# A merged out-projection and FFN head: turns set between products, masks in banks of their own, rows split ahead of the routing

## The chip, the cores and the metric

The kernel runs on one core of one Trainium2 chip. The metric is the device time of one launch in microseconds (us), as the median of several runs.

## The reference

Two transformer layers are computed over x of shape 4 x 512 x 512 (four batches of 512 tokens, width 512). Each layer is a cross-attention and a feed-forward block, each on a layer norm of x, with residual adds. This case touches the joint between the second layer's attention and its feed-forward block:

```python
attn = attn.reshape(b, n, N_HEADS * HEAD_DIM)
return attn @ Wout + bout                       # added to x
...
xf = layernorm(x).reshape(-1, d)
gate_base, up_base = xf @ Wg.T, xf @ Wu.T       # DFF = 1408
probs = softmax(xf @ Wr.T)                      # 8 experts
topw, topi = top_k(probs, 2)
# for each expert e, with weight we (zero where e is not chosen):
h = silu(gate_base + xf @ Ag_e.T @ Bg_e.T * 2) * (up_base + xf @ Au_e.T @ Bu_e.T * 2)
acc += (h @ Ad_e.T @ Bd_e.T * 2) * we           # rank 16
out = x + silu(gate_base) * up_base @ Wd.T + acc
```

## The kernel before

Each engine has its own list of instructions, written out by hand, and semaphores join the lists. A product of full precision is made from two halves: every operand is split in a high part (a copy by ACT, rounded to the type that TensorE reads) and a low part (a subtraction by DVE), and `product` runs three matmuls for each of four slices of the inner dimension, 12 in all, each 128x512. A block that must stand with its columns on the partitions is first "turned": four 128x128 transposes on TensorE into one PSUM bank, from which ACT and then DVE make the two halves.

The stage around the change is `phase_out_head`. A tile is 128 tokens; a batch has four tiles. The loop `for j in range(B + 2)` is a pipeline over the four batches:

- for batch j (while j < 4): `turn_rows` turns the four tiles of attention output, `row_hi` (ACT) and `row_lo` (DVE) split them into `aT`, `out_product` multiplies with Wout into the banks `y0` and `y1`, DVE adds to x (`add`) and takes statistics (`add_stats`, `variance`), ACT takes the root (`deviation`), DVE the `reciprocals`, and POOL writes the normalised rows (`normalise`) over `wout_raw`.
- for batch j-1: `turn_x`, `normed_hi`, `normed_lo` turn and split the normalised rows into `late_xnT`; `router` multiplies with Wr, `copy_router` and `turn_logits` bring the logits back to tokens on partitions, and `route` (DVE, 21 short instructions, with two exponentials of ACT, `gaps`, among them) picks the two experts and writes `hots`.
- for batch j-2: `turn_hots`, `hot_rows_hi` and `hot_rows_lo` turn that choice, `masks` spreads it by four small products to four masks of 128x512, ACT copies them (`copy_masks`), `lora_rows` multiplies the rows with Ag and Au into the banks `a0` and `a1`, DVE multiplies them with two of the masks (`mask_rows`), and ACT and POOL split the result (`masked_hi`, `masked_lo`).

With j = 4 and j = 5 no out-projection is left, and `prep` turns and splits the first slice of FFN weights at j = 4. The turns of rows and of x share the two banks `tp0` and `tp1`, and the masks of before use them too. The sync engine (SP) issues all DMAs of the stage in a fixed order. An all-engine barrier ends the stage, and `phase_ffn1` follows: 44 steps of matmuls over slices of DFF, whose products go through a ring of three banks and are summed by DVE into x and into `down_acc`, which lies in the memory of `attn`, and was first cleared there.

In the traces `attn` is also the memory of the attention rows, the masks, the masked rows and the raw weights; `late_weights` holds `aT`, `sel` and the turned choice besides the FFN weights; `wout_raw` holds the normalised rows.

## Time and profile before

| | |
|---|---|
| median of 3 runs | 1816.04 us (1815.12 to 1817.34) |
| profiled execution, its own time | 1813.96 us |
| its span | 1811.4 us |
| mean granted TensorE clock | 0.942 of full speed |
| TensorE busy over the span | 1632.4 us (90%) |
| VectorE (DVE), ScalarE (ACT), GpSimd (POOL) busy | 1059.8, 786.7, 460.1 us |
| `phase_out_head` in the trace | 1060.8 us to 1217.6 us |

The profile names a group by the line of the kernel, the engine, the operation and the tiles (out<-in). All products have line 48 or 56, the helpers, so they are told apart by their tiles: `h_y` is the out-projection, `h_a` the adapter rows, `h_r` the router, `h_tp` and `h_m` are turns and masks, `f_...` belongs to `phase_ffn1`. Idle time is given with what ended it.

### The profile page before, as it was taken

To read this page: it belongs to the slowest core of one execution; us is meant where nothing else is said; L and a number is where in the kernel's file an instruction comes from. 1 tells how busy PE (TensorE), PEld (TensorE's weight loads), DVE (VectorE), ACT (ScalarE), POOL (GpSimd) and SP (SyncE) were. 2 spreads that over 40 slices of the span, in tenths; PEclk is the share of its full clock that TensorE was granted. 3 is DMA by queue.
4 is the path that set the end of the run, shared out by engine and by line. 5 is a ranking of instruction groups with operands and counts; after the bars stand their busy time and mean duration, and the time that the engine had idled before them with its cause. 6 is when DMAs were issued, how large, how long until landed. Compare 5 with 4: busy or idle time off the path is not lost. (4 is left out here: it accounts for less than half of the span.)

```text
span 1811.4 us, 25116 instructions
## 1 busy us (share of the span) xinstructions
PE 1632.4 (90%) x8534; PEld 1197.8 (66%) x8534; DVE 1059.8 (59%) x1957; ACT 786.7 (43%) x1239; POOL 460.1 (25%) x425
## 2 busy tenths in 40 slices
PE   6988599999767869999999987969999999999996
PEld 5767599999745643343334355647888888888885
DVE  5886622222166748889998835534555556544545
ACT  4663223323244316877887852443333333223321
POOL 1210123322155650111110010242322232333331
PEclk9999599999978877999999998889999999999998
DMA  8995135562165572222222211332333336422211
GB/s 283 342 376 188 36 124 208 215 225 82 53 232 163 186 198 54 72 72 72 70 66 66 51 19 47 138 134 96 125 125 97 111 120 280 145 82 70 78 54 58
DMA packets 109515, 236.12 MB, mean 130 GB/s; under 512 B 39808, under 2 KB 53248, under 8 KB 100688
## 3 DMA queue, kind: packets, MB, share of 16 engines
q1 hardware_dynamic: 103152, 214.06, 35.1%
q0 software_dynamic: 6240, 20.45, 3.3%
q8 instruction: 73, 1.20, 0.3%
q14 instruction: 50, 0.41, 0.1%
HBM read 274.71 MB, written 93.32 MB: 203 GB/s over the span
## 5 line engine op out<-in xcount | busy, mean ns | idle before, releaser
L1937 DVE TENSOR_REDUCE r_top<-r_ring 128x1 f32<-128x512 f32 x512 | 324.1, 682 | 35.9 <-PE r_ring L1834 31.6
L1920 ACT ACTIVATE r_probs<-r_st 128x1024 f32<-128x1024 f32 x256 | 248.1, 1022 | 49.8 <-PE r_st L1821 47.3
L2824 DVE TENSOR_TENSOR attn<-attn,f_u 128x512 f32<-128x512 f32 x132 | 90.8, 688 | 193.9 <-PE f_u L48 133.5
L48 PE MATMUL m_bank<-w_place,m_xT 128*128 x936 | 168.1, 329 | 3.6 <-issue 1.7
L2750 ACT ACTIVATE attn<-f_g 128x512 f32<-128x512 f32 x132 | 79.0, 599 | 183.9 <-PE f_g L56 124.1
L48 PEld LDWEIGHTS m_bank<-w_place,m_xT 128*128 128x128 f32 x936 | 153.4, 191 | 7.8 <-issue 4.5
L1855 PE MATMUL r_out<-r_probs,early_v 128*17 128x512 f32 x1024 | 136.4, 605 | 0.5 <-ACT r_probs L1920 0.4
L2779 POOL TENSOR_TENSOR wout_split<-attn,wout_split 128x512 fp32r<-128x512 f32 x66 | 85.7, 1298 | 196.2 <-ACT wout_split L2754 196.2
L2779 POOL TENSOR_TENSOR f_hidS<-attn,f_hidS 128x512 fp32r<-128x512 f32 x66 | 85.6, 1297 | 194.8 <-ACT f_hidS L2754 194.8
L48 PE MATMUL f_g<-late_xnT,late_weights 128*128 128x512 f32 x528 | 129.5, 395 | 5.0 <-PEq L2064 5.0
L48 PE MATMUL f_u<-late_xnT,late_weights 128*128 128x512 f32 x528 | 129.4, 394 | 0.0
L1834 PE MATMUL r_ring<-early_slots 48*128 48x512 f32 x256 | 108.2, 507 | 17.5 <-PEq L1281 12.9
L2792 DVE TENSOR_TENSOR x_tokens<-f_ring,x_tokens 128x512 f32<-128x512 f32 x176 | 120.2, 692 | 0.0
L48 PEld LDWEIGHTS f_g<-late_xnT,late_weights 128*128 128x128 f32 x528 | 100.7, 191 | 26.4 <-issue 5.4
L48 PEld LDWEIGHTS f_u<-late_xnT,late_weights 128*128 128x128 f32 x528 | 97.7, 188 | 19.8
L1834 PEld LDWEIGHTS r_ring<-early_slots 48*128 48x128 f32 x256 | 44.9, 196 | 99.1 <-DVE r_top L1937 81.2
L1834 PE MATMUL r_ring<-r_kM,r_qS 48*128 48x512 f32 x256 | 104.8, 480 | 2.8 <-DVE r_top L1937 0.5
L1743 POOL TENSOR_TENSOR attn<-r_sums,r_rinv 128x256 f32<-128x256 f32 x32 | 19.9, 622 | 337.3 <-DVE r_rinv L1953 337.3
L1194 DVE TENSOR_TENSOR m_hT<-m_bank,m_hT 128x384 fp32r<-128x384 f32 x39 | 21.8, 558 | 137.8 <-ACT m_hT L1027 109.2
L1834 PEld LDWEIGHTS r_ring<-r_kM,r_qS 48*128 48x128 f32 x256 | 43.4, 189 | 86.4 <-DVE r_top L1937 79.8
L48 PE MATMUL m_bank<-w_place,m_hT 128*128 (+1 forms) x351 | 90.8, 403 | 1.4 <-DVE m_hT L1194 1.4
L834 POOL DMA_INDIRECT y_rows<-m_rows,m_scatter_at x39 | 38.6, 990 | 187.5 <-ACT m_rows L1034 187.5
(330 smaller groups left out, 3076.0 us busy)
## 6 DMA issues: line engine op xcount, KB each, us to landing
w_place<-expert_split SPq DMA_DIRECT2D x72, 1408.0 KB
w_place<-expert_split SPq DMA_DIRECT2D x36, 1024.0 KB
late_w_dram<-late_weights SPq DMA_DIRECT2D x11, 1920.0 KB
expert_split<-w_place SPq DMA_DIRECT2D x10, 1408.0 KB, 9.4
w_place<-expert_split SPq DMA_DIRECT2D x36, 384.0 KB
late_weights<-late_w_dram SPq DMA_DIRECT2D x11, 1024.0 KB
late_weights<-late_w_dram SPq DMA_DIRECT2D x11, 896.0 KB
early_slots<-y_rows SPq DMA_DIRECT2D x16, 512.0 KB
```

What stands on the lines that cost most here:

```text
L48: last = nc.tensor.matmul(out, l, r, start=(i == 0), stop=(i == len(passes) - 1))
L834: nc.gpsimd.indirect_dma_start(y_rows, bass.IndirectOffsetOnAxis(scatter_at[:, i:i + 1], 0), rows[:, XS + i % YS, :], None).then_inc(y_out ...
L1194: nc.vector.tensor_tensor(hT[:, i % 2, LO], bank[1][:, 0:FT * P].rearrange("p (j c) -> p j c", j=FT), fp32(hT[:, i % 2, HI]), ALU.subtract ...
L1743: nc.gpsimd.tensor_tensor(fp32(attn[:, b * KT:(b + 1) * KT, at:at + GROUP * HD]).rearrange("p t (h c) -> p t h c", h=GROUP), sums[g % 2][: ...
L1834: nc.tensor.matmul(ring(place(q, h))[:], qS[s][rows, h // 2, q * P:(q + 1) * P], kM[s][rows, h // 2, :], start=True, stop=True).then_inc(m ...
L1855: last = nc.tensor.matmul(out_ps[h * PAD:h * PAD + VCOLS, :], v[:, k, g, h * VCOLS:(h + 1) * VCOLS], probs[k][:, h, :], start=(k == 0), st ...
L1920: nc.scalar.activation(probs[k][:, 2 * pair:2 * pair + 2, :], st_ps[pair][:], ACT.Exp, scale=SCALE).then_inc(exp_done, 1)
L1937: nc.vector.reduce_max(top[g % 2][:, q, h:h + 1], ring(place(q, h))[:], AXIS_X).then_inc(max_read, 1)
L2750: nc.scalar.activation(hid[:, c, var, :], g_ps[c][:], ACT.Silu).then_inc(silu_done, 1)
L2779: nc.gpsimd.tensor_tensor(hidS[c][:, var, LO, :], hid[:, c, var, :], fp32(hidS[c][:, var, HI, :]), ALU.subtract).then_inc(hid_split, 1)
L2792: nc.vector.tensor_tensor(x[:, at, :], ring(use)[:], x[:, at, :], ALU.add).then_inc(y_added, 1)
L2824: nc.vector.tensor_tensor(hid[:, c, var, :], hid[:, c, var, :], u_ps[c][:], ALU.mult).then_inc(hid_done, 1)
```

## The change

Nothing is computed in another way, apart from the first sums of `down_acc`. What changes is the order in each engine's list, the banks of the masks, and some waits.

- The turns of x stand one by one between the products of the next batch, masks and adapter products instead of in a block of four, and the masks and the adapter rows of batch j-2 come before the router of batch j-1 instead of after it. At j = 5 the adapter rows come first.
- The masks use the banks `m` and `r` (which the turned choice and the router use) instead of `tp0`, `tp1` and `m`.
- `row_lo` for the first two tiles of the next batch stands ahead of `route` on DVE.
- The constants are turned after the second product of batch 0 instead of after the fourth.
- SP stores the masks of batch 2 ahead of the split weights, and no longer waits at the end of the stage for the masks to land; `phase_ffn1` waits for them instead, on SP before the first load of a mask and on ACT before its first step.
- In `phase_ffn1` the first sums into `down_acc` are written by a copy; the memset that cleared it is gone, and DVE's wait for it.

```diff
-        mask_ps = (tp[0], tp[1], m_ps, tp[0])
+        mask_ps = (m_ps, r_ps, m_ps, r_ps)
...
+            store_masks(2)
             sp.wait_ge(prep_split, late.PARTS)
             late.store_split(sp, 0)
-            store_masks(2)
             store_masks(3)
-            sp.wait_ge(mask_out, B * DMA)
...
# PE, turn_rows(j, t), t < 2
-                    wait_count(pe, mask_copied, 4 * (j - 2))
-                    wait_count(pe, x_split, TPB * (j - 1))
+                    wait_count(pe, rows_split, TPB * (j - 1) + t + 3)
+                    wait_count(pe, x_split, TPB * (j - 2) + t + 3)
# PE, turn_x(j, t), t < 2
-                    pe.wait_ge(rows_split, TPB * min(j + 2, B))
-                    if j + 1 >= B:
-                        pe.wait_ge(mask_copied, 4 * (j - 1))
+                    pe.wait_ge(rows_split, min(TPB * (j + 1) + t + 3, TILES))
+                    wait_count(pe, x_split, TPB * (j - 1) + t + 3)
# PE, router(j)
+                wait_count(pe, mask_copied, 4 * j)
# PE, masks(j, *ks)
-                        pe.wait_ge(x_split, TPB * min(j + 2, B))
-                        wait_count(pe, mask_copied, 4 * j)
-                    elif k == 3:
-                        pe.wait_ge(mask_copied, 4 * j + 1)
+                    elif k == 1:
+                        pe.wait_ge(logits_copied, j + 1)
+                    else:
+                        pe.wait_ge(mask_copied, 4 * j + k - 1)
...
# DVE, the loop's end at each j (before: route, row_lo, row_lo, mask_rows)
+                if routed:
+                    mask_rows(j - 2, 1)
+                if j == B:
+                    prep_lo(3)
                 if j + 1 < B:
                     row_lo(j + 1, 0)
                     row_lo(j + 1, 1)
-                if j >= 2:
-                    mask_rows(j - 2)
+                if normed:
+                    route(j - 1)
...
# ACT, the middle of the loop
+                if routed:
+                    copy_masks(j - 2, 0, 1)
+                if out_now:
                     deviation(j)
+                if j == B:
+                    prep_hi_of(1)
+                if normed:
+                    normed_hi(j - 1, 2)
...
# phase_ffn1
+            act.wait_ge(late.mask_out, B * DMA)
-            nc.gpsimd.memset(down_acc, 0.0).then_inc(acc_clear, 1)
...
-                nc.vector.tensor_tensor(acc, ring(use)[:], acc, ALU.add).then_inc(y_added, 1)
+                if step % STEPS_H < CH:
+                    nc.vector.tensor_copy(acc, ring(use)[:]).then_inc(y_added, 1)
+                else:
+                    nc.vector.tensor_tensor(acc, ring(use)[:], acc, ALU.add).then_inc(y_added, 1)
```

TensorE at j = 2, from the first product of batch 2 on, stands so before (`h_y` is a product of the out-projection, `h_tp<-identity,attn` a turn of attention rows, `h_tp<-identity,wout_raw` a turn of x, `h_m<-identity,h_hots` the turned choice):

```order
L48 MATMUL h_y1<-wout_split,late_weights 128x512 x12
L2178 MATMUL h_tp1<-identity,attn 128x128 x4
L48 MATMUL h_y0<-wout_split,late_weights 128x512 x12
L48 MATMUL h_y1<-wout_split,late_weights 128x512 x12
L2178 MATMUL h_tp0<-identity,wout_raw 128x128 x4
L2178 MATMUL h_tp1<-identity,wout_raw 128x128 x4
L2178 MATMUL h_tp0<-identity,wout_raw 128x128 x4
L2178 MATMUL h_tp1<-identity,wout_raw 128x128 x4
L2178 MATMUL h_m<-identity,h_hots 32x128 x4
L56 MATMUL h_r<-late_xnT,h_wrT 8x512 x12
```

and so in the changed kernel, from the third product to the turn that precedes the router:

```order
L48 MATMUL h_y0<-wout_split,late_weights 128x512 x12
L2177 MATMUL h_tp0<-identity,wout_raw 128x128 x4
L48 MATMUL h_y1<-wout_split,late_weights 128x512 x12
L2177 MATMUL h_tp1<-identity,wout_raw 128x128 x4
L2240 MATMUL h_m<-late_weights 128x512
L2240 MATMUL h_r<-late_weights 128x512
L48 MATMUL h_a0<-late_xnT,h_abT 128x512 x12
L2177 MATMUL h_tp0<-identity,wout_raw 128x128 x4
L2240 MATMUL h_m<-late_weights 128x512 x2
L2240 MATMUL h_r<-late_weights 128x512 x2
L48 MATMUL h_a1<-late_xnT,h_abT 128x512 x12
L2177 MATMUL h_tp1<-identity,wout_raw 128x128 x4
```

The four turns of x have moved apart, and the masks (L2240) and both adapter products (`h_a`) now stand among them, ahead of the router.

DVE behind the routing of batch 0, from the end of j = 1 into j = 2, stands so before (`h_hots` is the end of `route`, `late_weights<-h_tp` is `row_lo`, `x_tokens<-h_y` the add of a product):

```order
L2466 TENSOR_TENSOR h_hots<-ht_hot,ht_w 128x4x8
L2468 TENSOR_TENSOR h_hots<-ht_hot,ht_w 128x4x8
L2412 TENSOR_TENSOR late_weights<-h_tp,late_weights 128x512 x2
L2417 TENSOR_TENSOR x_tokens<-h_y,x_tokens 128x512
L2412 TENSOR_TENSOR late_weights<-h_tp,late_weights 128x512
```

and so in the changed kernel, from the last split of x at j = 1 to the start of `route` (its first line is the copy of the logits):

```order
L2478 TENSOR_TENSOR late_xnT<-h_tp,late_xnT 128x4x128
L2470 RECIPROCAL h_rstd<-h_std 128x4
L2472 SCALAR_TENSOR_TENSOR h_shift<-h_moments,h_rstd 128x4
L2478 TENSOR_TENSOR late_xnT<-h_tp,late_xnT 128x4x128 x2
L2449 TENSOR_TENSOR late_weights<-h_tp,late_weights 128x512 x2
L2488 COPY h_logits<-h_r 128x32
L688 TENSOR_REDUCE ht_top<-h_logits 128x4
```

The two splits of the next batch's rows, which stood between the end of the routing and the first add, now stand ahead of the routing's first copy, and the `reciprocals` have moved ahead of the last two splits of x.

TensorE at the end of the stage, from the last router on, stands so before:

```order
L2249 MATMUL h_r<-identity,h_rl 128x8 x4
L48 MATMUL h_a<-late_xnT,h_abT 128x512 x24
L2178 MATMUL h_m<-identity,h_hots 32x128 x4
L2241 MATMUL h_tp<-late_weights 128x512 x2
L2241 MATMUL h_m<-late_weights 128x512 x2
L2241 MATMUL h_tp<-late_weights 128x512 x2
L48 MATMUL h_a<-late_xnT,h_abT 128x512 x24
```

and so in the changed kernel:

```order
L2248 MATMUL h_r<-identity,h_rl 128x8 x4
L48 MATMUL h_a<-late_xnT,h_abT 128x512 x24
L2177 MATMUL h_m<-identity,h_hots 32x128 x4
L2240 MATMUL h_m<-late_weights 128x512
L2240 MATMUL h_r<-late_weights 128x512
L2240 MATMUL h_m<-late_weights 128x512 x2
L2240 MATMUL h_r<-late_weights 128x512 x2
```

Before, the first of the two groups of `h_a` belongs to batch 2 and the last to batch 3; now batch 2's has gone ahead of the last router, and batch 3's comes before its masks.

## Rows read from the trace of the kernel before

**Rows 1.** Windows: each stretch's length, busy time of each engine, PEclk, DMA share, GB/s.

```profile
1060.00:1217.50 157.50, 123.54 (x551) 89.84 (x551) 77.54 (x213) 53.50 (x98) 32.52 (x33) 0.88 0.25 91
1217.50:1811.40 593.90, 576.46 (x2574) 474.82 (x2574) 312.35 (x468) 185.74 (x309) 174.82 (x133) 0.98 0.32 112
```

**Rows 2.** Waits from 1060 to 1217.5: total us, times, longest us.

```profile
PE h_y L48 <- DVE late_weights L2412: 8.3, 3, 4.8
PE h_tp L2178 <- DVE late_xnT L2441: 7.3, 4, 2.0
```

**Rows 3.** Timeline of TensorE, batch 0: start us, us busy, then the group.

```profile
1067.61 3.02 PE L48 MATMUL h_y<-wout_split,late_weights 128*128 128x512 f32 x12
1070.47 0.60 PE L2178 MATMUL h_tp<-identity,attn 128*128 128x128 f32 x4
1070.82 5.72 PE L48 MATMUL h_y<-wout_split,late_weights 128*128 128x512 f32 x24
```

**Rows 4.** Timeline of ACT.

```profile
1071.11 0.60 ACT L2306 ACTIVATE late_weights<-h_tp 128x512 fp32r<-128x512 f32 x1 [2.61 <-PE h_tp L2178]
...
1131.44 1.28 ACT L2310 ACT_TABLE_LOAD   x1
```

**Rows 5.** Timeline of DVE.

```profile
1071.74 0.69 DVE L2412 TENSOR_TENSOR late_weights<-h_tp,late_weights 128x512 fp32r<-128x512 f32 x1 [0.38 <-ACT late_weights L2306]
...
1094.01 0.69 DVE L2417 TENSOR_TENSOR x_tokens<-h_y,x_tokens 128x512 f32<-128x512 f32 x1 [1.30 <-PE h_y L48]
...
1095.96 0.17 DVE L2429 TENSOR_SCALAR h_var<-h_moments 128x4 f32<-128x4 f32 x1
...
1105.96 0.19 DVE L2451 COPY h_logits<-h_r 128x32 f32<-128x32 f32 x1 [5.73 <-PE h_r L2249]
...
1110.99 1.29 DVE L2412 TENSOR_TENSOR late_weights<-h_tp,late_weights 128x512 fp32r<-128x512 f32 x2
...
1224.55 0.69 DVE L2787 TENSOR_TENSOR late_weights<-f_prep,late_weights 128x512 fp32r<-128x512 f32 x1 [10.62 <-ACT late_weights L2739]
```

**Rows 6.** Timeline of TensorE from the first router on.

```profile
1100.05 4.78 PE L56 MATMUL h_r<-late_xnT,h_wrT 128*8 128x512 f32 x12 [1.50 <-DVE late_xnT L2441]
1105.51 0.41 PE L2249 MATMUL h_r<-identity,h_rl 8*128 8x8 f32 x4 [0.68 <-ACT h_rl L2328]
...
1111.74 5.49 PE L48 MATMUL h_y<-wout_split,late_weights 128*128 128x512 f32 x12 [4.79 <-DVE late_weights L2412]
...
1163.36 5.28 PE L56 MATMUL h_r<-late_xnT,h_wrT 128*8 128x512 f32 x12 [0.97 <-issue]
...
1186.42 2.94 PE L56 MATMUL h_r<-late_xnT,h_wrT 128*8 128x512 f32 x12 [1.02 <-issue]
...
1191.38 5.75 PE L48 MATMUL h_a<-late_xnT,h_abT 128*128 128x512 f32 x24
...
1204.20 8.40 PE L48 MATMUL h_a<-late_xnT,h_abT 128*128 128x512 f32 x24
1217.58 5.46 PE L48 MATMUL f_g<-late_xnT,late_weights 128*128 128x512 f32 x12 [4.98 <-PEq L2064]
```

**Rows 7.** Timeline of POOL at the end of the stage.

```profile
1198.37 4.96 POOL L2400 TENSOR_TENSOR late_am<-attn,late_am 128x512 fp32r<-128x512 f32 x4 [15.94 <-ACT late_am L2350]
...
1214.07 2.49 POOL L2400 TENSOR_TENSOR late_am<-attn,late_am 128x512 fp32r<-128x512 f32 x2 [0.29 <-ACT late_am L2350]
1217.54 3.52 POOL L2774 MEMSET attn<- 128x4096 f32 x1 [0.98 <-POOLq L2064]
```

**Rows 8.** Windows of three short stretches, columns as in group 1.

```profile
1068.00:1070.00 2.00, 2.00 (x10) 1.62 (x9) 1.44 (x3) 0.49 (x1) 0.00 (x0) 1.00 0.00 0
...
1111.70:1114.00 2.30, 2.26 (x5) 1.84 (x6) 0.58 (x1) 0.00 (x0) 0.00 (x0) 0.50 0.03 7
...
1178.00:1180.50 2.50, 0.00 (x0) 0.00 (x0) 1.32 (x3) 2.15 (x4) 2.50 (x3) 1.00 0.00 0
```

**Rows 9.** DMA issues from 1055 to 1260: count, KB each, median us to landing.

```profile
late_mask_dram<-attn SPq DMA_DIRECT2D x4, 512.0 KB, 2.6
```

More of the change, by code:

```diff
@@ L2353, in _, with prep_hi_of @@
             row_hi(0, 1)
+            def prep_hi_of(part):
+                act.wait_ge(prep_turned, part + 1)
+                _, size, to = late.part(0, part)
+                nc.scalar.activation(to[HI], y_ps[part % 2][:, 0:size], ACT.Copy).then_inc(prep_hi, 1)
             for j in range(B + 2):
-                if j < B:
+                out_now, normed, routed = j < B, 1 <= j <= B, j >= 2
+                if out_now:
                     row_hi(j, 2)
@@ L2503, in _ @@
                         nc.vector.tensor_tensor(to[LO], bank, fp32(to[HI]), ALU.subtract).then_inc(const_split, 1)
-                if j == B:
-                    for part in range(late.PARTS):
-                        dve.wait_ge(prep_hi, part + 1)
-                        _, size, to = late.part(0, part)
-                        nc.vector.tensor_tensor(to[LO], y_ps[part % 2][:, 0:size], fp32(to[HI]), ALU.subtract).then_inc(prep_split, 1)
-                if 1 <= j <= B:
-                    for t in range(TPB):
-                        normed_lo(j - 1, t)
-                if j >= 2:
-                    hot_rows_lo(j - 2)
-                if j < B:
-                    reciprocals(j)
-                if 1 <= j <= B:
-                    route(j - 1)
+                if routed:
+                    hot_rows_lo(j - 2)
+                if out_now:
+                    add(j, 2)
+                    add_stats(j, 2)
+                if normed:
+                    normed_lo(j - 1, 0)
+                if out_now:
+                    add(j, 3)
+                    add_stats(j, 3)
+                    variance(j)
+                if normed:
+                    normed_lo(j - 1, 1)
+                if j == B:
+                    prep_lo(0)
+                if out_now:
+                    reciprocals(j)
+                if j == B:
+                    prep_lo(1)
+                if normed:
+                    normed_lo(j - 1, 2)
+                if routed:
+                    mask_rows(j - 2, 0)
+                if j == B:
+                    prep_lo(2)
+                if normed:
+                    normed_lo(j - 1, 3)
+                if routed:
+                    mask_rows(j - 2, 1)
+                if j == B:
+                    prep_lo(3)
                 if j + 1 < B:
@@ L2621, in _ @@
                 late.load_raw(sp, 1, part)
+            sp.wait_ge(late.mask_out, B * DMA)
             load_mask(0)
```

155 lines of the change are left out of this document (88 added, 67 removed).

## The prediction

> **What bounds the kernel now.** I began with the windows of the stage that the change rewrites and of the one behind it. From 1217.5 us on, TensorE is busy 576.46 of 593.90 us at a granted clock of 0.98 [rows 1]: matmuls alone set that end. In the stage before it TensorE is busy 123.54 of 157.50 us at 0.88. So it has 34 us without work, and some of its work runs at the lower clock. The waits say on what: 8.3 us in three waits of a product for `row_lo`, one of them 4.8 us, and 7.3 us in four waits for `normed_lo` [rows 2]. The rest are short ones and the tail.
>
> The timeline then shows the prices. At full clock a product starts 2.86 us before what follows it (1067.61 to 1070.47), a turn 0.35 us [rows 3]; for turns of x and of the choice I take 0.5, nearer to the 0.60 that a turn counts as busy. From the start of a turn to the end of its low half it is 0.64 us to ACT, 0.63 to DVE, 0.69 for DVE [rows 3 to 5]; with 0.05 for the semaphore a turn has its product ready 2.0 us after its start. That is the wait of 2.0 us in [rows 2]: four turns of x in two banks have nothing to hide it.
>
> The worst place is behind the first router. It ends at 1104.83 (1100.05 + 4.78), and the next product starts at 1111.74, after an idle wait of 4.79 us: `row_lo` stands behind `route`, and `route` holds DVE from 1105.96 to 1110.99, 5.03 us [rows 5, 6]. When TensorE comes back, its clock is 0.50, that is 1.2 GHz [rows 8], and the product takes 5.49 us where one at 2.4 GHz takes 3.02: 2.4 us more.
>
> **The change part by part.** I walk the new order with these durations. Clock 0 is a router's end.
>
> *A turn of the loop with j = 2 or 3.* The logits are turned at 0.68 (the wait for `copy_router`) and take 0.37 [rows 6]. Nothing of DVE is then waited for: product 0 starts at 1.05. `row_lo` of the second tile ends at 1.95, and `route` runs from there to 7.0. TensorE meanwhile does two products, two turns of rows and the turned choice: 1.05 + 2.86 + 0.36 + 2.86 + 0.36 + 0.5 = 8.0. The third product needs the third `row_lo`, behind `route` and one add: 7.0 + 2 x 0.69 = 8.4, a wait of 0.4. Then product, turn of x, product: 14.6; turn of x and two masks: 15.7; the first adapter product, 2.8 us (half of 5.75 [rows 6]): 18.5; a turn, two masks of two matmuls, the second adapter product: 23.1. The last turn of x starts there and nothing but one turn of rows covers its 2.0 us, so the router starts at 25.1 and ends 2.9 later at 28.0. Two such turns of the loop take 56.0 us.
>
> ACT has to keep up: the variance is ready 2.1 us after the last product's end (1094.01 to 1096.13 [rows 5]), at 16.8; ACT is then at the first two masks until 17.1, loads its table for the root in 1.28 us [rows 4], and the third turn of x, at 18.5, is copied at 19.2, on time. This chain is 0.5 us from being late.
>
> Before, the same stretch, from the first router's end to the third's, is 1104.83 to 1168.64 (1163.36 + 5.28), 63.8 us [rows 6]. It held the masks and adapter rows of one batch, and the new one holds those of two. **Term A: 56.0 - 63.8 = -7.8 us.**
>
> *j = 4.* Here a wait arises that was not there. The turned choice needs `route`, which now has no products in front of it: `route` runs from 1.05 to 6.1 and TensorE has only the logits, so it sits idle from 1.05 to 6.15. Behind the choice in its list stand two turns of x, `prep`, the masks and the adapter product of batch 2, and the last router; all of them wait. Before, the masks and adapter product of batch 1 and `prep` filled that time. From 6.15: choice and two turns 1.5, `prep` 0.5, then masks at 8.4 once ACT and DVE have split the choice, 0.6, `prep` 0.5, adapter 2.8, turn 0.5, masks 1.2, `prep` 0.5, adapter 2.8, last turn at 17.3, 2.0 us of split, router from 19.3 to 22.2. An idle stretch of 5.1 us is longer than the one that had the clock fall before, so I add 1.9 us, the excess of the first router (4.78 against 2.94 [rows 6]): 24.1 us. Before it was 1168.64 to 1189.36, 20.7. **Term B: +3.4 us.**
>
> *j = 5 and the tail.* Before, behind the last router stand masks and logits (2.0 us), the adapter rows of batch 2 (to 1197), the choice, masks, and the adapter rows of batch 3 at 8.40 us, of which 2.65 is the low clock [rows 6]; then `mask_rows`, ACT and POOL in turn, until the first matmul of the next stage at 1217.58: 28.2 us. Now: adapter rows from 1.05 to 6.6, choice turned by 7.1, its halves at 8.5, the first two masks copied at 10.2, all four at 11.75 with ACT's copies at just under the 0.60 of [rows 4] each. `mask_rows` starts at 10.3; ACT's first high half waits for its mask copies and ends at 12.4; POOL's four low halves take 4.96 [rows 7]: 17.4, and the barrier and code change take 1.0 (1216.56 to 1217.58 [rows 6, 7]): 18.4. POOL, not TensorE, ends the stage. **Term C: 18.4 - 28.2 = -9.8 us.**
>
> *Ahead of the first router.* The constants are now turned at about 1070.8. Their DMAs have landed: from 1068 to 1070 nothing moves [rows 8]; had they not, the two products behind would wait. In exchange the variance of batch 0 comes 1.8 us later, but the table load that ACT had ahead of it is done by then, so the first product of batch 1 is 0.3 us late. In j = 1 the last two turns of x still wait for `variance`, `deviation` and each other; I get the router's start at 99.8 (1099.8 us) against 1100.05. Taken with the same low clock: **Term D: -0.25 us.**
>
> *The rest is hidden.* SP passes the mask store ahead of the split-weights store: it waits for masks that are there 5 us before `prep` is done. The waits for landed masks: the last copy is at 11.75 and a mask lands in 2.6 us [rows 9], 14.4 against POOL's 17.4; without that cover it would cost up to 2.6 us. The memset ran for 3.52 us on POOL [rows 7], but DVE's first work behind it is at 1224.55 [rows 5], so its loss frees nothing; had DVE been waited for there, it would have been worth those 3.5 us. Eight copies in place of eight adds shorten DVE by at most their own 0.69 us each, 5.5 us in all, on an engine busy 312 of 594 us beside a TensorE that is busy 97% [rows 1]: 0, and 5.5 us as the far end that I don't believe.
>
> **Sum:** -7.8 + 3.4 - 9.8 - 0.25 = -14.45 us. The profiled execution took 1813.96 us, 2.1 below the median of 1816.04, so it becomes 1799.5, and the median 1801.5.
>
> The unknown cost is the clock. Its best case: no fall at the first router (1.9), none at j = 4 (1.9), none at the next stage's first product (2.4 of 5.46): -20.7, so 1795.4. Its worst: a fall in each loop turn with j = 2, 3, where I count 1.5 to 2 us of idle time (2 x 2.4), and 0.05 us more in some fifteen handoffs: -8.9, so 1807.1.
>
> A rule of the Trainium skill speaks against the new order. First the rows: around 1178 us TensorE had nothing but turns and waits, and yet its clock was 1.00 with 2.5 us idle [rows 8], and the router behind took the 2.94 us of full clock [rows 6]. "TensorE: Matmul & The Clock Gate", Part 4: PE-mode transpose, says that transposes don't count as busy time for releasing the clock the way matmuls do. By that rule the turns with which j = 4 restarts would not bring the clock back, and the first adapter product would run at 1.2 GHz too; by the rows they hold a clock that is up. No row here shows turns alone raising it.
>
> **The rivals.**
> - *Low clock after the restart at j = 4 (rival 1).* The first adapter product pays what the product at 1111.74 paid, 2.4 us, and the masks with it: 1803.9 to 1806. For it: the stretch opens with turns after the longest idle wait. Against: the row at 1178. That is the rule above. Chance 0.15, inside my range.
> - *The new order hides more (rival 2).* No fall of the clock: 1795.4, and less where the tail's ACT and POOL overlap better. Against: the waits of 5.1 and 2.0 us remain. Chance 0.09.
> - *The change doesn't do what it says (rival 3).* Waits merely move: ACT's `deviation` stands ahead of the third `normed_hi`, and beyond its 0.5 us of slack each late us delays both later turns of x and the router. Late by 5 us in each of two loop turns and in j = 1, the gain is 0: 1816. For it: one engine's late work now blocks three batches. Against: ACT is busy 53.5 of 157.5 us [rows 1]. Chance 0.04.
> - *Slower (rival 4).* Between products now stand turns, masks with one matmul and short waits; if these keep the clock at 1.2 GHz throughout j = 2 and 3, eight products, two routers and four adapter products lose about 2.4 us each, 34 us, and the result is 1835; it decides against the change from six of the fourteen on. Against: before, single turns between products kept full clock, 2.86 us a product [rows 3]. Chance 0.03.
> - *The forecast*, 1796 to 1804: 0.69.
>
> **How the numbers follow.** The range 1796 to 1807 joins forecast and rival 1 (0.84) and leaves out rivals 3 and 4, and most of rival 2. About 0.2% (3.6 us) is what a measurement can tell from no change: faster takes forecast, rivals 1 and 2, 0.93; same 0.04; slower 0.03.
>
> **What would show it.** The next profile should show `phase_out_head` about 143 us long; no wait of a product for `row_lo` above 1 us behind the first three routers; `route` starting behind two `row_lo`; an idle stretch of about 5 us ahead of the turned choice at j = 4, with the clock at 0.50 behind it; router to router 28 us twice, then about 24, then 18.4 to the first `f_g`; and the last stage as long as before, 594 us. The prediction is wrong if the clock stays low in the loop, if DVE or ACT is late for the third turn of x, or if the barrier waits for something other than POOL.

## The result and the profile after

The changed kernel ran at a median of 1809.45 us (1805.12 to 1812.64, six runs); beside it the kernel before had 1815.8 us (1813.89 to 1819.91, six runs). The ratio is 0.9956, with a 95% interval of 0.9941 to 0.997: some 8 us, or 0.3 to 0.6%, faster. The prediction was 1801.5 us with a range of 1796 to 1807. The direction was right, the gain about half of what was forecast, and the median lies outside the range. One execution in this whole study, of the run x9, took 2640.93 us at a mean granted clock of 0.553 and is left out everywhere.

The profiled execution took 1809.97 us, its span is 1808.2 us, its mean granted clock 0.942. The windows of the stage and of what follows it, columns as in [rows 1]:

```profile
1066.80:1214.50 147.70, 117.76 (x551) 86.61 (x551) 81.87 (x213) 53.70 (x98) 32.19 (x32) 0.89 0.27 97
1214.50:1808.20 593.70, 575.79 (x2574) 474.34 (x2574) 312.27 (x468) 185.36 (x309) 171.26 (x132) 0.98 0.33 112
```

The last stage is as long as before (593.9 in [rows 1]), the rewritten one 9 us shorter. It also starts 6.0 us later than in the profile of before (1066.81 against 1060.78), though nothing ahead of it was changed; identical code entered it between 1060.8 and 1066.8 us in the profiles of this study. So I compare within the stage, from its first turn on. DVE's busy time grew from 77.54 to 81.87 us with the same 213 instructions: some of them take longer. POOL still ends the stage.

The waits of TensorE in the stage (total us, times, longest us):

```profile
PE h_m L2177 <- DVEq L2506: 8.6, 3, 6.7
PE h_y L48 <- DVE late_weights L2449: 4.1, 3, 2.8
PE h_r L56 <- issue: 3.6, 3, 1.5
PE h_tp L2177 <- DVE late_xnT L2478: 2.3, 2, 2.0
```

The waits of products for `row_lo` fell from 8.3 to 4.1 us, those of the turns of x from 7.3 to 2.3 [rows 2]. In their place the turned choice now waits 8.6 us for `route`, 6.7 of them at j = 4.

TensorE's timeline at the places of [rows 6]: behind the first router, at j = 4, and the end:

```profile
1106.43 2.93 PE L56 MATMUL h_r<-late_xnT,h_wrT 128*8 128x512 f32 x12 [0.58 <-DVE late_xnT L2478]
...
1110.38 3.02 PE L48 MATMUL h_y<-wout_split,late_weights 128*128 128x512 f32 x12
...
1145.41 0.61 PE L2177 MATMUL h_m<-identity,h_hots 128*32 128x128 f32 x4 [0.62 <-DVEq L2506]
1146.79 3.06 PE L48 MATMUL h_y<-wout_split,late_weights 128*128 128x512 f32 x12 [0.77 <-DVE late_weights L2449]
...
1174.18 1.03 PE L2177 MATMUL h_m<-identity,h_hots 128*32 128x128 f32 x4 [6.67 <-DVEq L2506]
1175.00 1.91 PE L2177 MATMUL h_tp<-identity,wout_raw 128*128 128x128 f32 x8
...
1179.61 4.36 PE L48 MATMUL h_a<-late_xnT,h_abT 128*128 128x512 f32 x12
...
1190.76 2.93 PE L56 MATMUL h_r<-late_xnT,h_wrT 128*8 128x512 f32 x12 [1.13 <-issue]
...
1201.79 0.61 PE L2177 MATMUL h_m<-identity,h_hots 128*32 128x128 f32 x4 [1.35 <-DVEq L2506]
...
1214.57 5.46 PE L48 MATMUL f_g<-late_xnT,late_weights 128*128 128x512 f32 x12 [7.17 <-PEq L2064]
```

Behind the first router the product starts 1.02 us after the router's end (1109.36 to 1110.38) and runs at full clock, where it had waited 4.79 us and then taken 5.49. At j = 4 the idle stretch is 6.67 us, not 5.1, and what follows is at half clock at first. The window of that restart, columns as above:

```profile
1174.50:1177.00 2.50, 2.50 (x14) 2.37 (x13) 0.95 (x2) 1.24 (x3) 0.00 (x0) 0.50 0.50 210
```

Measured stretch by stretch from these timelines (router ends, `r0` to `r3`; us):

| | before | predicted | after |
|---|---|---|---|
| stage's start to r0 | 44.05 | 43.80 | 42.55 |
| r0 to r1 (j = 2) | 30.37 | 28.0 | 27.77 |
| r1 to r2 (j = 3) | 33.44 | 28.0 | 29.30 |
| r2 to r3 (j = 4) | 20.72 | 24.1 | 27.26 |
| r3 to first `f_g` | 28.22 | 18.4 | 20.88 |
| stage | 156.80 | 142.35 | 147.76 |

### Where the missing microseconds went

DVE's timeline at the start of `route` at j = 4, and POOL's at the same time:

```profile
1163.91 0.68 DVE L2513 SCALAR_TENSOR_TENSOR attn<-h_a,attn 128x512 f32<-128x512 f32 x1
...
1167.83 0.18 DVE L688 TENSOR_REDUCE ht_top<-h_logits 128x4 f32<-128x32 f32 x1
1168.09 0.86 DVE L690 TENSOR_TENSOR ht_score<-h_logits,ht_top 128x32 f32<-128x32 f32 x1
1169.03 1.15 DVE L693 TENSOR_TENSOR ht_score<-ht_score,h_rev 128x32 f32<-128x32 f32 x1
1170.25 0.19 DVE L695 TENSOR_REDUCE ht_best<-ht_score 128x4 f32<-128x32 f32 x1
...
1171.30 0.19 DVE L690 TENSOR_TENSOR ht_score<-ht_rest,ht_top 128x32 f32<-128x32 f32 x1
```

```profile
1162.88 2.55 POOL L2437 TENSOR_TENSOR late_am<-attn,late_am 128x512 fp32r<-128x512 f32 x2
1167.65 2.48 POOL L2437 TENSOR_TENSOR late_am<-attn,late_am 128x512 fp32r<-128x512 f32 x2 [2.22 <-ACT late_am L2369]
```

L690 and L693 take 0.86 and 1.15 us; the same L690 takes 0.19 three microseconds later. POOL runs two instructions of `masked_lo` (L2437) from 1167.65 to 1170.13, so the first ends near 1168.9. L690 ends at 1168.95 and L693 at 1170.18: each ends with a POOL instruction. L688, a reduction with one input, takes its 0.18 beside the same POOL instruction, and `mask_rows` at 1163.91, one of whose operands lies in PSUM, its usual 0.68 beside an earlier one. So do routes 1, 2 and 3 stretch, to 6.45, 6.54 and 6.9 us, while route 0, which has no `masked_lo` beside it, takes 4.9; before, all four took 4.91 to 5.24.

In the old order `mask_rows` stood behind `route` on DVE, so ACT and POOL split the masked rows when `route` was over. In the new order `mask_rows` stands ahead of it, and POOL's last two subtractions of a batch fall on the start of `route`.

This is a rule that the prediction had not weighed. "SBUF — State Buffer" in the Trainium skill, section "SBUF: two separate sides", says that DVE and GpSimd share a pair of SBUF ports under an exclusive lock that is held for a whole instruction, and that a DVE instruction with two SBUF inputs wants it against a GpSimd instruction that reads SBUF; the other "fully blocks". The rows above agree in all three points: the two instructions that are held have two inputs in SBUF, they are held for what is left of POOL's instruction (1.25 us), and a one-input one is not held. Whether it costs TensorE as much as it costs DVE is what the experiments had to tell.

### The profile page after: what moved, and what is told of

Its sections match the earlier page's. It is cut to its first block and busy times, and to the rows that moved or that the text cites. A ratio compares the mean times of both kernels' runs of the same rounds, so it can differ in the third digit from the quotient of the medians.

```text
span 1808.2 us, 25118 instructions
## 1 busy us (share of the span) xinstructions
PE 1627.4 (90%) x8534; PEld 1196.0 (66%) x8534; DVE 1066.2 (59%) x1957; ACT 786.5 (43%) x1239; POOL 455.5 (25%) x424
## 5 line engine op out<-in xcount | busy, mean ns | idle before, releaser
L48 PEld LDWEIGHTS f_u<-late_xnT,late_weights 128*128 128x128 f32 x528 | 97.7, 188 | 19.8
```

What stands on the lines that cost most here:

```text
L48: last = nc.tensor.matmul(out, l, r, start=(i == 0), stop=(i == len(passes) - 1))
```

## The experiments

Theories after the first comparison: (T1) POOL beside `route` costs some 1.6 us three times over, and all three are on the path at j = 3, 4 and 5; (T2) the wait at j = 4 and the low clock behind it are a price of the order itself; (rival) a lengthened `route` is a symptom, and the loss is TensorE's clock or the changed order of ACT. The kernel before had 1816.77 us (11 runs) beside x1 to x4, 1818.98 (20 runs) beside x5 to x8 and 1818.79 (11 runs) beside x9 to x11. So versions of different groups are compared by their ratios to it, and differences within the stage come from one profile each.

### x1: the kernel before once more

> The kernel before, profiled once more. In the first two profiles phase_out_head is 156.8 us before and 147.8 us after, 9.0 us less, but the changed kernel also enters the stage 6.0 us later, in code that is the same. If that is chance (theory), this profile enters the stage somewhere between 1058 and 1068 us, and its stage is 156.8 +- 1.5 us long. If the change itself delays the earlier stages (rival), it enters at 1060.8 +- 1 us again.

Measured: 1816.62 us (one run), span 1814.5, the stage 156.94 us from 1063.67 on; every stretch within 0.06 us of the first profile. So the theory holds: between these two executions the stage is the same, and the time of entry differs by 2.9 us.

### x2: POOL's last two subtractions wait for the route

```diff
 # POOL, masked_lo
                 for q in range(4):
+                    if q == 2 and j + 2 <= B:
+                        pool.wait_ge(hots_made, j + 2)
                     pool.wait_ge(am_hi, 4 * j + q + 1)
```

> The changed kernel; POOL holds the last two low halves of each batch's masked rows until the routing that runs beside them has written its choice. Theory: POOL's subtractions block DVE's two-input instructions in route (0.77 to 0.89 and 1.15 to 1.18 us where the same ones take 0.19), which makes three of the four routings about 1.6 us longer; so route for batches 1, 2 and 3 falls from 6.5 us to 5.0, TensorE waits less for the turned choice, by about 1.4, 1.5 and 1.4 us, and the kernel gains 3 to 5 us on the changed one, 12 to 14 on the one before. Rival (ACT's masked_hi and its table load, or the stores of DMAs, stretch route): the long instructions stay, and the gain is 0.

Measured: 1802.19 us (1799.35 to 1808.18), ratio 0.993 (0.9912 to 0.9948); stage 140.63 us, 7.1 shorter than after. The stretches are 42.51, 27.71, 28.03, 23.86 and 18.52. The first rows are DVE's, the last POOL's, for the same place as above:

```profile
1163.07 0.19 DVE L690 TENSOR_TENSOR ht_score<-h_logits,ht_top 128x32 f32<-128x32 f32 x1
1163.34 0.19 DVE L693 TENSOR_TENSOR ht_score<-ht_score,h_rev 128x32 f32<-128x32 f32 x1
```

```profile
1167.54 2.50 POOL L2439 TENSOR_TENSOR late_am<-attn,late_am 128x512 fp32r<-128x512 f32 x2 [7.15 <-DVEq L2508]
```

The routes are back at 4.9, 5.2, 4.9 and 5.22, with ACT's list untouched, so the rival is out. Nothing but POOL's start was moved, by a wait more, and the stage is 7.1 us shorter: 1.3 at j = 3, 3.4 at j = 4, 2.4 at the end. That is more than the 4.6 us by which three routes shrank (6.45 + 6.54 + 6.9 against 5.2 + 4.9 + 5.22). Of the 3.4 us at j = 4, 1.6 lie ahead of the turned choice and belong to the route. The other 1.8 lie behind it, where the clock came up sooner, and they can't be credited to the edit: x5 and x6 below waited 6.67 and 6.66 us for the choice, as after did, and took no longer from there than x2 (17.71 and 17.09 us against 17.75; after 19.51). In the time of the whole kernel the gain on after is some 5 us by the ratios (0.9956 to 0.993), but the intervals overlap. Four of the five stretches are now what the prediction gave, within 0.3 us. T1 holds for the routes and for what waits for them.

### x3: at j = 4 batch 2's adapter rows first

```diff
 # PE
-                if j > B:
+                if j >= B:
                     lora_rows(j - 2, 0)
...
-                if routed and j <= B:
+                if routed and j < B:
                     lora_rows(j - 2, 0)
...
-                if routed and j <= B:
+                if routed and j < B:
                     lora_rows(j - 2, 1)
```

> The changed kernel; at j = 4 both adapter products of batch 2 stand ahead of the turned choice, as they do at j = 5. Theory: the wait of 6.7 us ahead of the turned choice at j = 4, and the low clock behind it, are the largest cost of the change; 5.6 us of work fill the wait, the clock stays at full speed, and router to router at j = 4 falls from 27.3 us to 18 to 20; the gain on the changed kernel is 6 to 9 us. Rival (the split of x and of the weights on ACT and DVE bounds j = 4, not the wait): the router starts at the same distance, and the gain is below 2 us.

Measured: 1802.92 us (1799.83 to 1805.46), ratio 0.9924 (0.9908 to 0.9939); stage 140.30. TensorE at j = 4:

```profile
1166.38 5.76 PE L48 MATMUL h_a<-late_xnT,h_abT 128*128 128x512 f32 x24
1173.19 0.61 PE L2177 MATMUL h_m<-identity,h_hots 128*32 128x128 f32 x4 [1.05 <-DVEq L2506]
...
1181.85 4.33 PE L56 MATMUL h_r<-late_xnT,h_wrT 128*8 128x512 f32 x12 [2.38 <-issue]
```

The two adapter products fill the wait (6.67 to 1.05 us), their time is no longer spent behind it, and the turns run at full clock: r2 to r3 goes from 27.26 to 20.81. That is just outside the 18 to 20 that I expected, with a router at partly low clock (4.33). T2 holds too: with the stretched routes in place the order at j = 4 costs 6.5 us against after, and 4.0 to 4.7 us against x6 and x5, where the clock came up sooner (24.84 and 25.46).

### x4: both edits

> The two edits together. Theory: the wait for the choice at j = 4 is then covered in full; the gains add except for the 1.5 us of routing at j = 4 that each of them hides: 9 to 12 us on the changed kernel, 17 to 21 on the one before, a median near 1797. If the two compete for one bound, it is no better than the better of the two.

Measured: 1795.93 us (1794.91 to 1804.16), ratio 0.9892 (0.9873 to 0.9911); stage 135.61, 12.2 shorter than after. The two edits give 7.1 and 7.5 alone, so 2.4 us are common to them: with the adapter rows in front, TensorE waits for a long `route` less. By the ratio that is some 20 us under the kernel before, as expected, and its interval lies below those of both kernels.

### x5: POOL work put beside route 0

Five small POOL subtractions on data that nobody else needs start with the first routing, the only one that was undisturbed:

```diff
 # POOL, the loop
             for j in range(B + 2):
+                if j == 2:
+                    pool.wait_ge(logits_copied, 1)
+                    ... # five subtractions of 128x192, from h_const_raw and h_spare to h_spare
```

> The changed kernel, and beside the first routing, the one routing that has no work of POOL beside it, POOL does five small subtractions of 192 columns on a spare tile, whose result nobody uses. Theory (POOL's reads of SBUF block DVE's instructions with two inputs in SBUF): instructions of route that take 0.19 us now take up to 0.5 us more while POOL works, the routing of batch 0 grows from 4.9 us to between 5.8 and 7, and router to router at j = 2 from 27.7 to between 28.3 and 29.5; the one-input reductions stay at 0.19. Rival (ACT or DMAs stretch the others): the routing stays at 4.9.

Measured: 1804.05 us (one run); route 0 takes 5.51 us instead of 4.9, the others 6.45, 6.55 and 6.92 as after. Router to router at j = 2 is 28.35 us against 27.77. DVE and then POOL:

```profile
1107.27 0.38 DVE L690 TENSOR_TENSOR ht_score<-h_logits,ht_top 128x32 f32<-128x32 f32 x1
1107.72 0.19 DVE L693 TENSOR_TENSOR ht_score<-ht_score,h_rev 128x32 f32<-128x32 f32 x1
...
1110.21 0.57 DVE L2499 TENSOR_TENSOR ht_gap<-ht_top 128x4 f32<-128x4 f32 x1
```

```profile
1107.00 0.60 POOL L2443 TENSOR_TENSOR h_spare<-h_const_raw 128x192 f32<-128x192 f32 x1 [3.77 <-DVE h_logits L2495]
1107.74 3.01 POOL L2446 TENSOR_TENSOR h_spare<-h_spare,h_const_raw 128x192 f32<-128x192 f32 x4
```

The effect appears where there was none, so its cause is POOL and not the batch. L690 ends at 1107.65, just behind POOL's first (1107.60), and L2499 at 1110.78, just behind its last (1110.75). But it is smaller than I had put it (5.8 to 7 us). Seven more two-input instructions lie between them and take 0.19: three of them began 0.12 to 0.14 us before one of POOL's ended, and four within 0.02 us of the start of one. POOL's last four took 0.64 to 0.66 us each where its first took 0.60, with 0.14 us between them, so nothing here shows it held for long either. What POOL costs DVE is thus not its busy time beside it (some 3.2 us here, for 0.6 us of route). What the rows show is that a two-input instruction that starts inside one of POOL's ends just behind it, so the price is at most one POOL instruction (0.60 against 1.25 us). Whether POOL waits when DVE is first, these rows don't settle.

### x6: the rows split behind the routing again

```diff
 # DVE, the loop's end (ACT's list stays that of the changed kernel)
-                if j + 1 < B:
-                    row_lo(j + 1, 0)
-                    row_lo(j + 1, 1)
                 if normed:
                     route(j - 1)
+                if j + 1 < B:
+                    row_lo(j + 1, 0)
+                    row_lo(j + 1, 1)
```

> The changed kernel with route ahead of the two splits of rows on DVE again; all else as in the changed kernel. Theory: the first product of batches 2 and 3 waits for route and one split, 5.8 us and 7.4 us, and comes back at 1.2 GHz (2.4 us); the 0.4 to 1.4 us of waits behind them vanish: 12 to 17 us slower than the changed kernel, so slower than the kernel before, 1821 to 1826. Rival (the splits hardly matter, since the masks and adapter rows now cover the routing): within 3 us of the changed kernel.

Measured: 1822.85 us (1819.69 to 1828.35, ten runs), ratio 1.0025 (1.0014 to 1.0037): slower than before, and by the ratios some 12.5 us slower than after, as the theory had it. The stretches are 45.17, 35.73, 37.44, 24.84 and 20.91. TensorE behind the first router:

```profile
1116.50 5.45 PE L48 MATMUL h_y<-wout_split,late_weights 128*128 128x512 f32 x12 [5.81 <-DVE late_weights L2449]
```

Each of the two loop turns loses 8 us. Without this part the rest of the change is a loss.

At j = 4 this run shows one thing more. The wait for the turned choice is the one of after (6.66 us), but the clock came back much sooner. TensorE, and the windows behind the wait, columns as above:

```profile
1190.52 1.04 PE L2177 MATMUL h_m<-identity,h_hots 128*32 128x128 f32 x4 [6.66 <-DVEq L2506]
1191.35 1.92 PE L2177 MATMUL h_tp<-identity,wout_raw 128*128 128x128 f32 x8
1193.05 0.80 PE L2177 MATMUL h_y<-identity,attn 128*128 128x128 f32 x4
...
1194.85 3.01 PE L48 MATMUL h_a<-late_xnT,h_abT 128*128 128x512 f32 x12
```

```profile
1190.50:1193.40 2.90, 2.88 (x14) 2.69 (x15) 1.01 (x2) 1.29 (x3) 0.00 (x0) 0.50 0.52 215
1193.50:1196.00 2.50, 2.50 (x14) 1.79 (x13) 1.57 (x4) 2.45 (x5) 0.00 (x0) 1.00 0.00 0
```

TensorE did nothing but turns until 1193.78, where the masks begin, and its clock was up by 1193.50, 2.9 to 3.0 us behind the wait; the first adapter product ran in 3.01 us, where after has 4.36.

### x7: the first sums by memset and add again

The FFN part of the change is undone, with the memset and DVE's wait for it as before. POOL waits for the stored masks first, since SP no longer does so at the end of the stage:

```diff
 # phase_ffn1: POOL, then DVE
+            pool.wait_ge(late.mask_out, B * DMA)
+            nc.gpsimd.memset(down_acc, 0.0).then_inc(acc_clear, 1)
...
-                if step % STEPS_H < CH:
-                    nc.vector.tensor_copy(acc, ring(use)[:]).then_inc(y_added, 1)
-                else:
-                    nc.vector.tensor_tensor(acc, ring(use)[:], acc, ALU.add).then_inc(y_added, 1)
+                nc.vector.tensor_tensor(acc, ring(use)[:], acc, ALU.add).then_inc(y_added, 1)
```

> The changed kernel with the FFN part undone: POOL clears the sums, DVE waits for that, and all first sums are added. Theory: TensorE bounds that stage and the memset is hidden, so no difference, the stage behind the barrier 593.6 +- 0.5 us. Rival (the shorter copies are worth something): up to 5 us slower than the changed kernel.

Measured: 1810.81 us (1806.01 to 1813.91), ratio 0.9953 (0.9935 to 0.9971), against 0.9956; the last stage 593.87 us against 593.63. No difference. But the stage of this profile took 152.48 us instead of 147.76, and 4.5 of these 4.7 us lie ahead of the first router's end, at 47.05 instead of 42.55. TensorE, the first product of batch 1:

```profile
1086.44 5.49 PE L48 MATMUL h_y<-wout_split,late_weights 128*128 128x512 f32 x12 [2.79 <-DVE late_weights L2449]
```

In the profile of after the same wait of 2.79 us was followed by a product of 3.06. See x9.

### x8: on the kernel before, only the rows split ahead of the routing

```diff
 # DVE of the kernel before (and row_hi ahead of gaps on ACT)
-                if 1 <= j <= B:
-                    route(j - 1)
                 if j + 1 < B:
                     row_lo(j + 1, 0)
                     row_lo(j + 1, 1)
+                if 1 <= j <= B:
+                    route(j - 1)
```

> The kernel before with one edit: the two splits of rows ahead of route on DVE (and ahead of the exponentials on ACT). Theory: only the first routing is exposed in the old order, since the adapter products stand in front of the next products at j = 2; its product comes 3.8 us earlier and at full clock, 5 to 7 us in all, and the rest stays: about 1810.5. If each routing of j = 1 to 3 counted alike it would be 15 us or more; if the split ahead of route only delays the routing and the products behind it, 0 to 2 us.

Measured: 1812.4 us (1808.44 to 1816.83, twelve runs), ratio 0.9963 (0.9953 to 0.9974); stage 151.75, 5.05 shorter. TensorE behind the first router:

```profile
1114.16 3.06 PE L48 MATMUL h_y<-wout_split,late_weights 128*128 128x512 f32 x12 [0.97 <-DVE late_weights L2412]
```

The wait of 4.79 us and the low clock behind it are gone. The first turn of the loop went from 30.37 to 26.52 us, though its router ran at low clock this time (5.28 against 2.95 us); the second went from 33.44 to 31.19, and there the low router had stood before. This part alone gives nearly what the whole change gives in time (0.9956); its interval and that of after overlap.

### x9: the changed kernel once more

> The changed kernel once more. Its two relatives with the same first 45 us of the stage showed the first router's end at 45.2 and 47.1 us after the stage's start where the changed kernel had 42.6, with the clock fallen behind the idle wait ahead of batch 1's first product. My theory, that this fall comes by chance, expects the stage at 147.8 us or at about 152, whichever way it falls, everything behind the first router as before within 0.3 us (27.8, 29.3, 27.3, 20.9), and a ratio to the kernel before of 0.994 to 0.997. The rival, that the first profile stands for all executions, expects 147.8 and 42.6 again.

Measured: 1808.23 us (1804.72 to 1811.64, five runs), ratio 0.994 (0.9923 to 0.9957); the profiled execution 1804.72 us, stage 147.08 us, with 41.83, 27.65, 29.31, 27.41, 20.88. The fall of the clock at batch 1 didn't show in this profile, so it alone tells nothing between theory and rival. Over all profiles in which that product waited 2.78 or 2.79 us it took 3.02 to 3.06 in six (after, x2, x3, x4, x5, x9) and 4.31, 5.49 and 5.49 in three (x6, x7, x10). The code ahead of it is the same in all nine. So the fall is not the edits' doing, and the first profile doesn't stand for all executions. What decides it is open: the three don't begin the stage as the six do throughout (in x7 and x10 the first product of batch 0 took 5.49 us, in x6 4.71, in the six 4.61 to 4.91).

### x10: DVE takes POOL's last four subtractions

```diff
 # POOL
-            for j in range(B + 2):
+            for j in range(B + 1):
...
 # DVE, behind mask_rows at j = 5, on top of x4
+                if j > B:
+                    for q in range(4):
+                        dve.wait_ge(am_hi, 4 * (B - 1) + q + 1)
+                        to = late.am[:, 1, q // 2, q % 2]
+                        nc.vector.tensor_tensor(to[:, LO, :], work[:, q, :], fp32(to[:, HI, :]), ALU.subtract).then_inc(am_split, 1)
```

> The kernel with both edits (POOL's last two low halves of a batch behind the route, batch 2's adapter rows first at j = 4), and at j = 5 DVE in place of POOL subtracts the four low halves of the last masked rows. Theory: POOL's four subtractions of 1.24 us each end the stage; DVE does each in 0.69 us, so the last router to the first product of the next stage goes from 19.1 to 16.5 us, the stage from 135.6 to about 133, the median some 2.5 us under that of the kernel with both edits, near 1793.5. Rival: ACT's high halves, each waiting for a multiplication by DVE, end the stage just before POOL does, and DVE, now with twelve instructions there in place of eight, delays them: less than 1 us of gain.

Measured: 1797.17 us (1792.41 to 1799.31), ratio 0.9868 (0.9852 to 0.9884). The last router to `f_g` takes 16.20 us, 2.87 less than x4. DVE, then TensorE:

```profile
1201.16 2.48 DVE L2576 TENSOR_TENSOR late_am<-attn,late_am 128x512 fp32r<-128x512 f32 x4
```

```profile
1088.78 5.49 PE L48 MATMUL h_y<-wout_split,late_weights 128*128 128x512 f32 x12 [2.79 <-DVE late_weights L2451]
...
1184.26 4.16 PE L56 MATMUL h_r<-late_xnT,h_wrT 128*8 128x512 f32 x12 [2.38 <-issue]
...
1204.62 4.31 PE L48 MATMUL f_g<-late_xnT,late_weights 128*128 128x512 f32 x12 [5.17 <-PEq L2064]
```

The theory's 2.5 us at the tail came, and the four took 2.48 where POOL's took 4.93; the rival's "less than 1 us" did not. The stage as a whole was longer than x4's (138.23 against 135.61), because the clock fell at two places: 4.4 us to the first router, 1.2 in the last. The median doesn't show the gain either; by the ratio it is 4 us (0.9892 to 0.9868), with overlapping intervals. So the tail is shown in the trace, and its worth in the time isn't settled.

### x11: and batch 1's first rows split ahead of batch 0's root

```diff
 # ACT
+                if j == 0:
+                    row_hi(1, 0)
+                    row_hi(1, 1)
                 if out_now:
                     deviation(j)
... # row_hi(j + 1, 0) and row_hi(j + 1, 1) where they stood:
-                if j + 1 < B:
+                if 0 < j < B - 1:
...
 # DVE
                     add_stats(j, 3)
+                    if j == 0:
+                        row_lo(1, 0)
                     variance(j)
...
-                    row_lo(j + 1, 0)
+                    if j:
+                        row_lo(j + 1, 0)
```

> The kernel of the run before, and for batch 0 row_hi of the next batch's first two tiles stands ahead of deviation on ACT, and the first row_lo ahead of variance on DVE. Theory: the idle wait of 2.8 us ahead of batch 1's first product shrinks to about 1 us, so the first router's end comes 1.8 us sooner (near 40.7 us after the stage's start), and without the long wait the clock has no place to fall there, so that end doesn't move to 45 or 47 us in any profile: stage near 131 us, median 1791 to 1792. Rival: the deviation and the normalised rows of batch 0 come later by as much, the turns of x wait for them, and the first router ends where it did: no gain over the run before.

Measured: 1792.21 us (1790.38 to 1795.11), ratio 0.9851 (0.9835 to 0.9867), the lowest here, though its interval overlaps that of x10; stage 134.58, not the 131 that I expected. TensorE:

```profile
1083.56 3.02 PE L48 MATMUL h_y<-wout_split,late_weights 128*128 128x512 f32 x12 [1.23 <-DVE late_weights L2454]
...
1101.21 4.10 PE L56 MATMUL h_r<-late_xnT,h_wrT 128*8 128x512 f32 x12 [0.45 <-DVE late_xnT L2483]
...
1176.30 5.28 PE L56 MATMUL h_r<-late_xnT,h_wrT 128*8 128x512 f32 x12 [2.38 <-issue]
```

The wait shrank from 2.79 to 1.23 us and the product kept full clock. The first router starts 38.01 us into the stage, against 39.62 in x4: 1.6 us sooner, so the rival (the turns of x take it back) is out. But I had expected that the clock had no place left to fall. It fell at the router itself, behind a wait of 2.02 us of the turn of x ahead of it, and again at the last router. The end of the first router, 42.11, is therefore only 0.45 us ahead of x4's.

## Why the prediction was wrong in size and right in direction

The sum was -14.45 us in the stage; the profile of after has -9.04. By the prediction's own steps:

**Term A (j = 2 and 3), -7.8 predicted, -6.74 measured: the mechanism right, one half mis-sized.** The turn of the loop with j = 2 took 27.77 us against 28.0: the walk over the new order was good to 0.3 us. At j = 3 it was 29.30: the choice waits 0.62 and the third product 0.77 us, behind a `route` of 6.45 us that I had put at 5.05. x2, with the route at 5.2, has 28.03.

**Term B (j = 4), +3.4 predicted, +6.54 measured: mis-sized.** I had named the wait, its place and its reason. The choice started 7.75 us after the router's end, not 6.15: 1.6 us from `route`. From there to the last router's end it took 19.5 us against 17.95, with 1.9 us for the clock in it: the turns, masks and first adapter product from 1174.18 to 1183.81 ran mostly at 1.2 GHz and took 9.6 us where the walk has 6.15, so the clock cost 3.5. That is rival 1, which I had held to 0.15 and dismissed by the row at 1178 [rows 8].

That dismissal was a misreading. The row shows TensorE without a single instruction, not turns that hold a clock. And the same trace has a stretch of turns and waits where the clock did fall, ahead of the first router (windows of the kernel before, columns: length, busy time of TensorE, PEclk, DMA share, GB/s):

```profile
1094.00:1097.20 3.20, 1.18 (x11) 1.00 0.00 0
1097.40:1100.00 2.60, 1.15 (x5) 0.50 0.00 0
```

But rival 1's own reason isn't shown either. Part 4 of "TensorE: Matmul & The Clock Gate" in the Trainium skill says that transposes don't count as matmuls do for the clock. The restart of after would fit that (2.5 us of turns without a gap at 0.50), the one of x6 doesn't: turns alone, and the clock up 2.9 us behind the wait. Behind a wait of 6.66 or 6.67 us the way from the choice to the last router's end took 19.5 to 19.8 us in three profiles (after, x7, x9) and 17.7 and 17.1 in two (x5, x6). So 1.6 us of this term's miss is the route, in every profile, and 1.6 is a clock that stayed down longer than the 1.9 us allowed for it, in three of five.

**Term C (tail), -9.8 predicted, -7.34 measured: mis-sized.** POOL ended the stage, as predicted (1208.63 + 4.93 = 1213.56, `f_g` 1.01 later). The choice started 8.10 us after the router's end instead of 6.6, again `route` (1.5 us), and behind idle waits of 1.35 and 1.48 us the masks ran at low clock; some 1.0 us more lies there. x2 has 18.52 in all, against 18.4.

**Term D, -0.25 predicted, -1.5 measured.** I had taken the first router at the low clock of before (4.78); it ran in 2.93. Whether that is the change or chance is open: with the old order of turns the first router took 4.78, 4.88 and 4.80 us (before, x1, x8), with the new one 2.92 to 2.95 in six profiles and 4.13 to 4.15 in three. Its end lay between 41.83 and 47.05 us in the nine profiles with this beginning. This term's honest value was a spread of some 5 us, and the range had none for it: I counted a fall there as a constant, and none at batch 1's first product.

The misses are +1.06, +3.14, +2.46 and -1.25, together 5.41, the whole of it. The step that failed is one assumption under terms A, B and C: that `route` keeps its duration (5.05 us in the walk) when it is moved beside POOL's `masked_lo`. It took 6.45 to 6.9 us there, and 4.9 to 5.2 again when x2 moved POOL away. Of the 6.66 us by which A, B and C missed, some 4.4 are this (1.3, 1.6 and 1.5). Most of the rest is the second mis-sized item, the clock's price, which I had set at 1.9 us at j = 4 and at nothing in the tail. I had asked of each moved instruction what it waits for and who waits for it, and not what runs beside it. None of the three signs that I had named for a wrong prediction came: the clock was up throughout j = 2 and 3, DVE and ACT were on time for the third turn of x, and POOL ended the stage.

**What was hidden** stayed hidden: the copy for the memset and adds (x7), and the waits for landed masks (the stage behind the barrier took 593.63 us against 593.82). Rival 3 didn't come: ACT was on time in both loop turns. Rival 4 didn't either: turns, masks and short waits between products kept full clock at j = 2 and 3 (product after product at 3.0). x6 and x8 add what the sum didn't separate: the split of rows ahead of the routing alone gives a ratio of 0.9963 where the whole change has 0.9956 and 0.994, and without it the rest is a loss (1.0025).

**What stays open.** Between the stage's gain in the profile (9.0 us) and the median's (6.4) lie the entry into the stage, which moved by up to 6 us in unchanged code, and the clock's falls; the ratios of after and x9, 0.9956 and 0.994, are 8 and 11 us. I made no run that settles what sets the entry time, or on which side of a short wait the clock falls. Nor was it tried whether the falls can be avoided by giving TensorE something to do in the waits of 2 to 3 us.

## What to carry to other kernels

When a change moves a chain of small DVE instructions, look at what POOL will do at that moment: a two-input instruction of 0.19 us took up to 1.18 us beside one of POOL of 1.25 us, and one wait more on POOL took at least 5 us out of the stage here. When a step is moved ahead, ask what else used to run beside the thing it overtakes: at j = 4 the adapter products were the cover of `route`, and putting them first again took another 5.0 us (x4 against x2) to 7.5 us (x3 against after) out of the stage. Idle stretches of TensorE of 2 to 3 us in front of products should be priced as a spread (0 to about 2.4 us each), not as a value.

## What the runs showed of the hardware that I had not expected

- A DVE instruction on 32 elements with two SBUF inputs took 0.77 to 1.18 us beside POOL subtractions of 1.25 us, and ended with them; one-input ones and those with one operand in PSUM kept their 0.19 and 0.68. Beside POOL instructions of 0.60 to 0.66 us two of nine were stretched, to 0.38 and 0.57.
- The same code with the same wait ahead of it ran at either clock level: after 2.79 us idle a product took 3.02 to 3.06 us six times, 4.31 once and 5.49 twice; after 2.38 us idle behind turns the last router took 2.94, 4.16, 4.33 and 5.28 (x4, x10, x3, x11). After 1.23 us the product took 3.02 (one profile), after 4.79 us 5.49 (the kernel before), after 5.81 us 5.45 (x6).
- The same list behind the same wait of 6.66 or 6.67 us brought the clock up at very different times: in x6 it was up 2.9 us behind the wait, with nothing but turns done since, and the adapter product took 3.01 us; in after the adapter product that began 5.4 us behind the wait still took 4.36 us.
